# GpSimd weights a pair's two one-hot tiles in two instructions instead of one

## The reference, cut to what matters

```python
deg = jax.ops.segment_sum(ew, col_f, num_segments=n)
norm = dinv[row_f] * ew * dinv[col_f]
h = x @ W
msg = h[row_f] * norm[:, None]
out = jax.ops.segment_sum(msg, col_f, num_segments=n)
```

## Time and profile before

| | |
|---|---|
| median of three runs | 589.72 us (587.36 to 590.27) |
| profiled execution, its own time | 589.59 us |
| its span, first to last instruction | 587.8 us |
| mean granted TensorE clock | 0.988 of full |
| PE busy | 551.5 us, 94% of the span |
| DVE busy | 466.7 us, 79% |
| ACT busy | 320.8 us, 55% |
| POOL busy | 283.7 us, 48%, of which L1028 89.4 us |
| chain that ended last | PE 66%, DVE 19%, issue 5%, ACT 5%, POOL 4% |

### The profile page before, as it was taken

The page is one execution under the profiler, slowest core; times in us unless marked ns, Lnnn a source line. Parts: engine busy times, 40 slices in busy tenths (PEclk is TensorE's granted clock), DMA queues, the critical chain, the costliest instruction groups (busy, mean ns, idle before and its releaser), DMA issues.

```text
span 587.8 us, 8713 instructions
## 1 busy us (share of the span) xinstructions
PE 551.5 (94%) x2921; PEld 451.3 (77%) x2921; DVE 466.7 (79%) x1049; ACT 320.8 (55%) x615; POOL 283.7 (48%) x317
## 2 busy tenths in 40 slices
PE   3888999999989999999999999999998999999997
PEld 2666888888878787888886766778876788788887
DVE  7978899989968688676998778668758786668985
ACT  6467889877855462213124765546455886423252
POOL 4664777777767414553843791002303673041562
PEclk9799999999989999999999999999999999999989
DMA  9400000000002021013004020000002000030004
GB/s 317 160 2 1 2 1 2 2 1 1 2 0 74 1 71 33 21 37 84 18 15 152 2 71 1 0 1 2 0 2 89 2 0 2 2 89 2 1 18 158
DMA packets 15079, 21.12 MB, mean 36 GB/s; under 512 B 3293, under 2 KB 6033, under 8 KB 15035
## 3 DMA queue, kind: packets, MB, share of 16 engines
q1 hardware_dynamic: 13674, 17.94, 9.6%
q10 hardware_dynamic: 1360, 2.62, 1.3%
HBM read 18.00 MB, written 2.56 MB: 35 GB/s over the span
## 4 chain that ended last, share of the span: by engine, by line
PE 66%; DVE 19%; issue 5%; ACT 5%; POOL 4%; DVEq 0%; POOLq 0%; ACTq 0%
PE p L2237 8%; PE p L2072 5%; PE pH L2088 5%; PE pQ L2088 4%; PE pQ L2357 4%; PE p L2357 4%; PE p L2088 4%; POOL qx L1209 2%; PE pH L2249 2%; DVE p L1512 2%; PE p L2322 2%; PE pH L2555 2%; PE pQ L2249 2%; PE pQ L2555 2%; POOL xT L1197 2%
## 5 line engine op out<-in xcount | busy, mean ns | idle before, releaser
L1028 POOL TENSOR_TENSOR Loh<-onehot,whl 128x512 fp32r<-128x512 bf16 x85 | 89.4, 1052 | 40.9 <-DVE onehot L1412 40.9
L2237 PE MATMUL p<-G,ATs 128*128 128x512 f32 x300 | 70.5, 391 | 0.0
L2237 PEld LDWEIGHTS p<-G,ATs 128*128 128x128 f32 x300 | 55.9, 188 | 11.6 <-issue 0.2
L2072 PEld LDWEIGHTS p<-Roh,Loh 128*128 128x128 f32 x340 | 50.5, 192 | 14.1 <-issue 6.6
L1412 DVE TENSOR_SCALAR onehot<-iota_src,srclo 128x128 bf16<-128x128 bf16 x170 | 57.5, 378 | 0.7 <-DVE flagint L1424 0.7
L2072 PE MATMUL p<-Roh,Loh 128*128 128x200 f32 x340 | 51.4, 274 | 2.8 <-DVE AT L1443 2.3
L2088 PE MATMUL pQ<-wsl,xT 128*128 128x512 f32 x168 | 49.2, 424 | 4.7 <-DVE xT L1316 2.6
L2088 PE MATMUL pH<-wsl,xT 128*128 128x512 f32 x168 | 47.8, 414 | 1.0 <-DVE xT L1316 1.0
L580 ACT ACTIVATE away<-iota_key,key 128x200 f32<-128x200 f32 x85 | 38.6, 454 | 13.6 <-PE p L2072 13.5
L1443 DVE TENSOR_TENSOR AT<-AT,p 128x200 f32 x85 | 30.1, 355 | 14.0 <-PE p L2072 12.5
L582 ACT ACTIVATE Roh<-away,onesf 128x200 fp32r<-128x200 f32 x85 | 39.4, 463 | 2.8
(11 more groups left out here) (659 smaller groups left out, 1445.7 us busy)
## 6 DMA issues: line engine op xcount, KB each, us to landing
xb<-in_x SPq DMA_DIRECT2D x9, 256.0 KB, 2.6
out<-nodes SPq DMA_DIRECT2D x9, 256.0 KB
raw<-in_L_mix_w_qkv SPq DMA_DIRECT2D x2, 1024.0 KB, 5.0
wraw<-in_L_mix_w_qkv ACTq DMA_DIRECT2D x2, 512.0 KB, 4.7
wraw<-in_L_mix_w_qkv ACTq DMA_DIRECT2D x1, 1024.0 KB, 8.7
nodes<-in_x SPq DMA_DIRECT2D x1, 1024.0 KB, 9.8
wraw<-in_L_mix_w_qkv SPq DMA_DIRECT2D x1, 1024.0 KB, 12.0
wraw<-in_L_gnn_W SPq DMA_DIRECT2D x1, 1024.0 KB, 14.2
```

The source lines that it names most:

```text
L1028: pool.tensor_tensor(Loh[:, g % SLOTS], o, w, ALU.mult).then_inc(S["oh_pool"], 1)
L2072: ins = pe.matmul(pW[g % 2][:, 0:T * WIN], Loh[:, g % SLOTS, c, part, :], roh(g, c), start=(c + part == 0), stop=(c + part == 2))
L2237: ins = pe.matmul(pG[u][:, :], ATs[:, u, x, s_, :], G[:, y, s_, :], start=(s_ + n == 0), stop=(s_ == T - 1 and n == 2))
```

## The change

The single TENSOR_TENSOR of 128x512 becomes two of 128x256, one for each column of the pair. The semaphore is raised by the second. The data written, the order and every other engine's instructions stay the same.

```diff
             for g in range(CP):
                 pool.wait_ge(S["oh_src"], g + 1)
-                w = whl[:, 2 * g:2 * g + 2, :].bitcast(F32).rearrange("p c (k n) -> p c k n", n=1).broadcast_to([P, 2, 2, P])
-                o = onehot_[:, g % SLOTS].rearrange("p c (k n) -> p c k n", k=1).broadcast_to([P, 2, 2, P])
-                pool.tensor_tensor(Loh[:, g % SLOTS], o, w, ALU.mult).then_inc(S["oh_pool"], 1)
+                for c in range(2):
+                    w = whl[:, 2 * g + c, :].bitcast(F32).rearrange("p (k n) -> p k n", n=1).broadcast_to([P, 2, P])
+                    o = onehot_[:, g % SLOTS, c].rearrange("p (k n) -> p k n", k=1).broadcast_to([P, 2, P])
+                    ins = pool.tensor_tensor(Loh[:, g % SLOTS, c], o, w, ALU.mult)
+                ins.then_inc(S["oh_pool"], 1)
```

## The result

Over 20 executions of each kernel the changed one takes 589.25 us in the median and the one before 587.75. The ratio is **1.0031, with a 95% interval of 1.0021 to 1.0041**: slower by 0.3%, 1.8 us. (The three executions shown ahead of the prediction, with 589.72 in the middle, lie high among the twenty, which go from 586.35 to 590.27; about 2 us of the distance between 592.1 and 589.25 is that.) The ratios of the experiments are against 17 executions of the kernel before (the first four) or 21 (the others), about 587.7 us in the median; two further ones, 685.53 and 902.2 us at a granted clock of 0.757 and 0.559, are left out. The profiled execution of the changed kernel has a span of 588.6 us against 587.8.

The account below looks back on a forecast made before the run. PE was taken as the bound in 57.5 to 171 us, DVE close behind; start 0.4, middle 1.8 and end 0.3 gave +2.5 us on 589.59, so 592.1 us, range 587.2 to 597.0.

Parts of the forecast that it names:

- The price of a half: POOL's 128x256 instruction: 0.62 us each, two queued 1.19, so +0.14 us of POOL time a pair.
- The turns alternate: Port shared by POOL and DVE: first one-hot goes between the halves, the second waits for the second half.
- The held pair, +0.08 us: Pair whose one-hots come in POOL's first half: cycle 1.42 us against 1.34, for 44 pairs.
- POOL's lost turn: Break between the halves: POOL loses 0.1 us to DVE's first one-hot, bounds 0 and 0.24.
- The pair that comes late, +0.14: Pair behind a residual, some 0.95 us after POOL's start: now meets the second half, +0.14 us, some 20 pairs.
- Start, +0.4: 50 to 57.5 us: four held pairs ahead of additions PE waits for, and a later first POOL end, +0.4 us.
- Middle, +1.8: PE's 9 stops for late additions, each with one or two held or late pairs in front, 0.2 us each.
- End, +0.3: DVE's run to the residual of 171.88, for which PE stands: three held pairs in front, +0.3 us.
- Rival 1: Both one-hots pass in the break between the halves: -3.5 us, 586.1 us; chance 0.14.
- Rival 2: POOL and the port become the bound, held pair cycling in 1.66 us against 1.44 granted: +17, 607 us; chance 0.10.
- Rival 3: Nothing changes, DVE's 9.1 us idle takes all 6.3 added: 589.7 us; chance 0.14.

Follow-up runs that it names:

- early cut: Two instructions a pair cut after 16 of the 128 places instead of between the columns, against the kernel before: 596.24 us, ratio 1.0139.
- filler in front: Kernel before with a tiny unused 128x1 POOL instruction between the wait for the one-hots and the whole instruction: 596.46 us, ratio 1.0146.
- right one-hot first: Kernel before, whole instruction kept, with DVE's right one-hot issued ahead of the two left ones: 600.31 us, ratio 1.0211.
- four quarters: Four POOL instructions of 128x128 per pair, each column and part by itself, against the kernel before: 595.89 us, ratio 1.0128.
- late cut: Two instructions a pair cut after 120 of the 128 places instead of between the columns, against the kernel before: 588.03 us, ratio 1.0000.
- filler behind: Kernel before with a tiny unused 128x1 POOL instruction behind each pair's whole instruction: 587.14 us, ratio 0.9996.

## Why the prediction was right and wrong

- *Direction and band*: slower by less than 0.5% was the likeliest case, and it came. But the forecast counted it as no change that could be told, since a measurement was said to tell 0.5%; over 20 executions of each kernel the interval is 0.2% wide, and 0.3% slower stands clear of it. 0.5% is about the scatter of the three executions shown ahead of it. The size was put too high: +2.5 us forecast, +1.8 by the ratio and +1.2 in the stage of the two profiled executions. Together with the high starting value, 592.1 became 2.9 us too much.
- *The price of a half*, 0.62 from the earlier trace rows: right, 0.617; two take 1.20, where 1.19 was forecast. The upper bound of dense inputs (0.738) was not needed.
- *The turns alternate*: right. The first one-hot took 0.33, the second 0.65 (forecast near 0.5 and up to 0.8). No second half was lengthened to 0.7, and DVE's idle time in the stretch fell from 9.1 to 7.4 us, not to some 4.
- *The held pair, +0.08 us*: **wrong, and this is the failed step.** I took 0.1 us for POOL's lost turn, between bounds of 0 and 0.24. It is 0: the second half takes 0.61. With that value, the sum I wrote gives 0.58 + 0.61 + 0.13 = 1.32 for the cycle against 1.34, so the usual held pair wins 0.02 instead of losing 0.08. What the one-hots lose over the stage, 3.4 us, is not in these pairs. The 0.1 was an estimate between its bounds, and the row behind the alternation has DVE operations of 0.7 us; that a one-hot of 0.24 is too short for POOL to lose by it is my reading, no run tried longer ones.
- *The pair that comes late, +0.14*: the place was right, the sizes were not. The 22 at 0.945 lose 0.06 and it costs nothing; the 9 at 0.5 to 0.9 lose 0.20 in their one-hots and 0.15 in the cycle, close to the 0.14 of the sum, but I had not set them apart. DVE got 3.4 us more in all, against 6.3 forecast.
- *Start, +0.4*: wrong, -0.06. It followed from the 0.08 of the held pair. *Middle, +1.8*: +0.97, and 12 stops instead of 9. The sum put 0.2 on each stop for held pairs and pairs behind a residual, and neither kind turned out to cost anything that shows; the time came from the nine pairs above. That the sign and half of the size came out is partly luck. *End, +0.3*: right, the stop grew from 2.04 to 2.28 us.
- *Rival 1*, both one-hots pass in the break: did not happen, though the first does. What the page SBUF — State Buffer of the Trainium skill states (section SBUF: two separate sides), an exclusive lock for the whole instruction, the traces agree with throughout: 1.04 us for a right one-hot of 0.31. It gives the pair to whoever issues first and does not spell out whose turn comes next when both engines wait, so it was no reason for this rival, as the prediction had it. By the prediction's own working that turn was worth the difference between a gain and a loss; no run here had both one-hots in the break to show it.
- *Rival 2*, POOL and the port as the bound: not at two instructions of equal size, but where the cycle of nearly all pairs passes 1.44 the time goes up: 1.49 with the early cut and +8.2 us, 1.49 with the filler in front and +8.6, 1.57 with the right one-hot first and +12.4. The edge that I named, 1.44, fits all runs (the four quarters, at 1.45, already cost 7.5 us); the split stays on the right side of it with 1.327 for half of its pairs.
- *Rival 3*, DVE's slack takes all: true, as far as the times tell, of the 22 late pairs and of the whole late cut, not of the split.

## What to carry to other kernels

Where two engines take turns at a shared port, look at the time from one start to the next of the engine whose instruction holds the other, sort it by when the other one comes, and compare it with what the bounding engine grants. The held time and the busy time of either engine do not tell what a change costs: 0.2 us of POOL was free behind the instruction and cost 8.6 us in front of it, and two kernels with equal POOL time differed by 8 us through the place of a cut alone. Before moving an instruction that never seems to wait, ask whether it is only placed where nobody could hold it.

## What the runs showed that I had not expected

The granted TensorE clock falls in some executions after PE's long stop at the end of the stage, and not in others. From 173 to 176 us, the kernel before, then the one with the filler behind, whose stops were 2.04 us in both:

```profile
173.00:176.00 3.00, 3.00 (x10) 2.52 (x10) 0.36 (x1) 0.00 (x0) 0.32 (x1) 0.50 0.00 0
```

```profile
173.00:176.00 3.00, 3.00 (x21) 2.68 (x20) 1.25 (x3) 0.00 (x0) 0.24 (x1) 1.00 0.02 5
```

At 0.50 of the full clock (1.2 in place of 2.4 GHz) 10 matmuls are recorded instead of 21 in the same 3 us, and from pair 79 to the last it takes 10.22 us instead of 8.63: 1.6 us, about as much as the whole effect of the change. The changed kernel shows the dip there in one profiled execution and not in the other, with a stop of 2.28 us in both; in the other it came from 57 us on, behind the stage's first pairs, for which PE waits. What decides it was not found. It is a reason to compare medians of many executions here, and stretches of the trace rather than spans.
